# Graph layers and mixture of experts on one core: set-up by column groups, ScalarE pairs with a bank of their own, degrees made early, and tile 0 multiplied between the last pairs

## What is computed

```python
x = x + gnn(layernorm(x), (src, dst), edge_weight)      # two graph layers
x = x + ffn(layernorm(x))                               # 16 experts, the best 2 of each row

# gnn: h [3125, 256], 50000 edges, sorted by dst
ew  = clip(abs(edge_weight), 1e-6)
deg = segment_sum(ew, dst) + 1
dis = rsqrt(deg)
for W, b, g, be in two layers:
    xw  = h @ W
    agg = segment_sum((dis[src] * ew * dis[dst])[:, None] * xw[src], dst) + dis**2 * xw + b
    h   = relu(layernorm(agg) * g + be) + h
# ffn: gate (256 -> 16), top 2, softmax over the two, relu MLP 256 -> 512 -> 256 per expert,
#      y = x + weighted sum, layernorm of y
```

## Time and profile before

| what | value |
|---|---|
| median of 3 runs | 1250.4 us (1247.85 to 1251.97) |
| the profiled execution | 1253.59 us |
| its span, first to last instruction | 1251.9 us |
| mean granted TensorE clock | 0.954 |
| PE busy | 1102.1 us (88%), 6433 instructions |
| DVE busy | 720.1 us (58%) |
| POOL busy | 608.7 us (49%) |
| ACT busy | 341.6 us (27%) |

### The profile page before, as it was taken

The page is one execution under the profiler, slowest core; times in us unless marked ns, Lnnn a source line. Parts: engine busy times, 40 slices in busy tenths (PEclk is TensorE's granted clock), DMA queues, the critical chain, the costliest instruction groups (busy, mean ns, idle before and its releaser), DMA issues. The chain is left out here.

```text
span 1251.9 us, 19252 instructions
## 1 busy us (share of the span) xinstructions
PE 1102.1 (88%) x6433; PEld 952.7 (76%) x6436; DVE 720.1 (58%) x1970; ACT 341.6 (27%) x794; POOL 608.7 (49%) x625
## 2 busy tenths in 40 slices
PE   1675789799999999997799999999994599999967
PEld 1453568588888888886588888888883599999954
DVE  8978668903444444342427777777777355454536
ACT  1538332401111121111101111111211133343337
POOL 3777777777777777770001111111112355555525
PEclk9999978799999999998899999999996799999988
DMA  7999700033433433213045544535447422222236
GB/s 282 335 392 389 309 2 1 8 106 106 157 107 117 147 107 111 101 54 105 0 176 178 202 155 150 202 126 193 146 146 247 145 73 73 69 73 73 72 106 234
DMA packets 76335, 180.75 MB, mean 144 GB/s; under 512 B 28930, under 2 KB 58252, under 8 KB 66508
## 3 DMA queue, kind: packets, MB, share of 16 engines
q1 hardware_dynamic: 44984, 151.67, 33.6%
q0 software_dynamic: 19776, 15.76, 4.6%
q10 hardware_dynamic: 11476, 12.07, 3.0%
HBM read 122.12 MB, written 57.33 MB: 143 GB/s over the span
## 5 line engine op out<-in xcount | busy, mean ns | idle before, releaser
L458 POOL DMA_INDIRECT weights_by_cell<-w_cell,cell x391 | 413.0, 1056 | 140.5 <-issue 136.1
L1148 PE MATMUL ps<-x_rows,w 128*128 128x256 f32 x1300 | 296.4, 383 | 7.4 <-DMA w<-weights_by_cell 7.1
L1148 PE MATMUL ps<-w 128*128 128x256 f32 x1300 | 301.1, 385 | 1.1 <-ACT w L850 1.1
L1148 PEld LDWEIGHTS ps<-x_rows,w 128*128 128x128 f32 x1300 | 248.0, 192 | 41.2 <-DMA w<-weights_by_cell 7.9
L1148 PEld LDWEIGHTS ps<-w 128*128 128x128 f32 x1300 | 243.4, 192 | 32.7 <-ACT w L850 2.6
L508 POOL DMA_INDIRECT token_and_home_of_slot<-pair,slot_id x50 | 49.6, 992 | 346.7 <-DVE slot_id L779 339.1
L606 DVE TENSOR_TENSOR layer<-ps,w 128x1024 bf16<-128x1024 f32 x87 | 105.0, 1216 | 26.2 <-PE ps L987 26.1
L1466 DVE TENSOR_SCALAR hidt<-ps,b1t 128x128 f32<-128x128 f32 x232 | 65.3, 344 | 90.6 <-PE ps L1322 90.6
L1334 PE MATMUL ps<-w,hidt 128*128 (+1 forms) x464 | 109.8, 380 | 0.0
L1322 PEld LDWEIGHTS ps<-xt,w1s 128*128 128x128 f32 x880 | 106.9, 192 | 2.8
L1322 PE MATMUL ps<-xt,w1s 128*128 128x128 f32 x880 | 107.1, 275 | 0.0
(11 more groups left out here) (237 smaller groups left out, 1371.3 us busy)
## 6 DMA issues: line engine op xcount, KB each, us to landing
w<-weights_by_cell SPq DMA_DIRECT2D x49, 1600.0 KB, 6.9
weights_by_cell<-w SPq DMA_DIRECT2D x26, 1600.0 KB, 8.4
w<-in_L_ffn_w_dram SPq DMA_DIRECT2D x32, 512.0 KB, 8.8
weights_by_cell<-w_cell,cell POOLq DMA_INDIRECT x391
w<-in_x_dram ACTq DMA_DIRECT2D x1, 3072.0 KB
hot<-in_x_dram ACTq DMA_DIRECT2D x24, 128.0 KB, 2.1
normalised_rows<-hot ACTq DMA_DIRECT2D x24, 128.0 KB, 4.7
out_dram<-w SPq DMA_DIRECT2D x24, 128.0 KB
```

What stands on the lines that cost most here:

```text
L458: pool.indirect_dma_start(adj[:, :], bass.IndirectOffsetOnAxis(ap=cell[0:m, c:c + 1].bitcast(U32), axis=0), w_cell[0:m, n, half * CH + j:h ...
L1148: mm = pe.matmul(bank(k % 2, 0, D), ring[:, place_of(k), s * P:(s + 1) * P], tab[q][:, s, :], start=(s == 0), stop=(s == NT - 1))
```

## The change

- **Set-up by column groups.** The four groups of 128 columns are set up one by one (`part(g, j)`, 25 operations each). Group 0 is made before the first pair; groups 1 to 3 stand two operations at a time in pairs 4 to 43. The first edges and weights have DMAs and semaphores of their own. The keys of a group are made by PE (a matmul with `pick`). The limits stand behind pair 1, and the last four operations of group 0 behind them. POOL waits for `part_ready` of the chunk's group.
- **28 pairs on ACT** (17 from pair 20 to 52, then every fourth), with a PSUM bank, a `same` slot and a semaphore of their own; the other 70 share two banks.
- **Degrees early:** three one-hot operations per pair (pairs 4 to 53); W1 from block 88 on, every second block; `tab[0]` scaled one tile per block from block 140.
- **Tile 0 of the first layer** is multiplied into bank 6 between the last pairs, one square every second block from block 144.
- SP waits for POOL's own DMAs (`seconds`) against two numbers from a table, and not for `placed`.
- The blank tile is half as wide and read twice per write.
- **Experts, end:** the gates are made in block 6 of the experts, and 12 diagonal pairs (8 of them in `w1s`) are filled before the last stage; the other 13 are made by halves, one or two per tile.

```diff
-KBANKS = 3
+KBANKS, ACT_BANK = 2, 2
-HOT_FIRST, HOT_STEP = 4, 2
+HOT_FIRST, HOT_STEP = 4, 3
-P_MEAN, P_PASSED, P_SHIFT, P_DEG = 12, 14, 31, HOT_LAST + 4
-T_APPLY, T_TAB, TAB_STEP, T_DEG, T_SCALE = 66, 84, 3, 2 * P_DEG, 2 * P_DEG + 6
-
-ACT_FIRST, ACT_LAST, ACT_STEP = 20, 64, 4
+P_MEAN, P_PASSED, P_SHIFT, P_DEG = 14, 14, 22, HOT_LAST + 4
+T_APPLY, APPLY_STEP, T_TAB, TAB_STEP, T_DEG = 46, 4, 88, 2, 2 * P_DEG
+T_SCALE = max(2 * P_DEG + 6, T_TAB + TAB_STEP * NT + 2)
+T_TILE, TILE_STEP = T_SCALE + 4, 2
+P_GUARD = T_APPLY // 2 + 2
+ACT_PAIRS = tuple(range(20, 54, 2)) + tuple(range(56, PAIRED - 1, 4))
+DVE_PAIRS = tuple(p for p in range(PAIRED) if p not in ACT_PAIRS)
+SIDE, PART_OPS, PART_SPAN = 6, 24, 13
+SECONDS = 16 * (CH * ((CHUNKS + 1) // 2) - 1)
...
+def part_pair(g, j):
+
+    return 4 + (g - 1) * PART_SPAN + j // 2 + (j >= SIDE)
...
-XRING, DIAGS = 3, 4
+XRING, DIAGS, OWN_DIAGS = 3, 12, 4
...
                     if q == 0:
-                        sp.reg_load(reg, chunks_of[0:1, t:t + 1])
-                        sp.wait_ge(placed, sp.snap(reg, min_val=1, max_val=CHUNKS + 1))
+                        for j in range(2):
+                            sp.reg_load(regs[j], second_need[0:1, j, t:t + 1])
+                        for j in range(2):
+                            sp.wait_ge(seconds[j], sp.snap(regs[j], min_val=16 * CH, max_val=SECONDS))
+                            sp.sem_inc(cells_blank, 1)
...
                 pool.wait_ge(limits_ready, 1)
-                pool.wait_ge(cols_ready, 1)
                 for n in range(CHUNKS + 1):
                     if n < CHUNKS:
                         if n == 0:
                             load_needs(0)
+                        pool.wait_ge(part_ready, (n * CH + CH - 1) // SH + 1)
                         pool.wait_ge(w_ready, n + 1)
...
+                for j in range(21):
+                    part(0, j)
+                dve.wait_ge(cols_ready, 1)
...
                 pair(0)
                 pair(1)
-                link(dve.tensor_copy(work_i[:, :], dst_c))
-                link(dve.tensor_scalar(work_i[:, :], work_i[:, :], 7, None, ALU.logical_shift_right))
-                link(dve.tensor_copy(dst_hi, work_i[:, :]))
+                limits()
                 weigh(0)
-                link(dve.scalar_tensor_tensor(dst_lo, dst_hi, -float(P), dst_c, ALU.mult, ALU.add))
+                limits_back()
+                for j in range(21, PART_OPS + 1):
+                    part(0, j)
...
+                    if s >= T_TILE and (s - T_TILE) % TILE_STEP == 0 and (s - T_TILE) // TILE_STEP < NT:
+                        n = (s - T_TILE) // TILE_STEP
+                        if n == 0:
+                            pe.wait_ge(deg_ready, 1)
+                            pe.wait_ge(loaded[place_of(0)], 16)
+                        pe.wait_ge(tab_ready[0], n + 1)
+                        mm = pe.matmul(bank(6, 0, D), ring[:, place_of(0), n * P:(n + 1) * P], tab[0][:, n, :],
+                                       start=(n == 0), stop=(n == NT - 1))
...
-                if t + DIAGS < NT:
-                    act.wait_ge(y_ps, t + 1)
-                    for k in range(2):
-                        ins = act.activation(diag[:, t % DIAGS, k, :], ident[:, :], ACT.Copy, scale=top_w[:, k, t + DIAGS:t + DIAGS + 1])
-                    ins.then_inc(diag_ready, 1)
+                for j in range(halves_by(t), halves_by(t + 1)):
+                    d, k = DIAGS + j // 2, j % 2
+                    act.wait_ge(y_ps, d - DIAGS + 1)
+                    ins = act.activation(diag(d, k), ident[:, :], ACT.Copy, scale=top_w[:, k, d:d + 1])
+                    if k == 1:
+                        ins.then_inc(diag_ready, 1)
```

More of the change, by code:

```diff
@@ L212, in gnn @@
         odd_need = sb("odd_need", [P, SC * P // CH], U16)
-        dst_c = setup(COLS)
         key = setup(COLS)
-        work = [setup(COLS) for k in range(4)]
-        work_i = sb("work_i", [P, COLS], I32)
+        hi_f, shi, at_cell, rest = (setup(P) for k in range(4))
+        v_i, s_i, d_i = (setup(P, I32) for k in range(3))
         cell = sb("cell", [P, COLS], I32)
@@ L587, in _ @@
-                link(dve.tensor_scalar(fourth[:, :], fourth[:, :], 0.0, None, ALU.is_equal))
-                for c in range(SC):
-                    ins = dve.tensor_scalar(begun[:, c, :], iota_vt[:, :], edge_hi[:, c, 0:1], fourth[:, 0:1], ALU.is_ge, ALU.mult)
-                ins.then_inc(limits_in, 1)
-                dve.wait_ge(limits_ps, 1)
-                did(dve.tensor_scalar(chunks_of[:, :], bank(7, 0, VT), 1.0, None, ALU.add))
-                link(dve.tensor_copy(top_v[:, 0, :], bank(7, BANK // 2, BANK // 2 + SC * P // CH)))
@@ new lines, in _, with limits @@
+                dve.wait_ge(consts, CONSTS)
+                for j in range(21):
+                    part(0, j)
+                dve.wait_ge(cols_ready, 1)
+                def limits():
+                    dve.wait_ge(late_consts, LATE_CONSTS)
+                    dve.wait_ge(ends_in, 16 * 5)
+                    did(dve.tensor_copy(end_dst[:, :, 0], ends_i[:, :, 0, 0]))
+                    link(dve.tensor_copy(end_dst[:, :, 1], ends_i[:, :, 1, 1]))
+                    link(dve.tensor_tensor(edge_v[:, :, :], end_dst[:, :, :],
+                                           block_row[:, :].rearrange("p (c k) -> p c k", k=1).to_broadcast([P, SC, 2]), ALU.add))
+                    link(dve.tensor_copy(edge_vi[:, :, :], edge_v[:, :, :]))
+                    link(dve.tensor_scalar(edge_vi[:, :, :], edge_vi[:, :, :], 7, None, ALU.logical_shift_right))
+                    link(dve.tensor_copy(edge_hi[:, :, :], edge_vi[:, :, :]))
+                    did(dve.tensor_scalar(chunk_hi[:, :], edge_hi[:, :, 1], VT - 1.0, None, ALU.min))
+                    link(dve.tensor_scalar(block_i[:, :], block_i[:, :], CH - 1, None, ALU.bitwise_and))
+                    link(dve.tensor_copy(fourth[:, :], block_i[:, :]))
+                    link(dve.tensor_scalar(fourth[:, :], fourth[:, :], 0.0, None, ALU.is_equal))
+                    for c in range(SC):
+                        ins = dve.tensor_scalar(begun[:, c, :], iota_vt[:, :], edge_hi[:, c, 0:1], fourth[:, 0:1], ALU.is_ge, ALU.mult)
+                    ins.then_inc(limits_in, 1)
@@ L974, in _, with turn_part @@
-                mm.then_inc(turned_w, 1)
+                def turn_part(g):
+                    at = (3 if g == 0 else 7) * BANK
+                    pe.wait_ge(cast_ready, g + 1)
+                    if g >= 2:
+                        pe.wait_ge(part_ready, g)
+                    for half in range(2):
+                        pe.transpose(ps[:, at + half * P:at + (half + 1) * P], e_f[:, g, half * P:(half + 1) * P], ident[:, :])
+                    pe.wait_ge(ends_ready, g + 1)
+                    for half in range(2):
+                        a = at + 2 * P + half * SH
+                        pe.matmul(ps[:, a:a + SH], key_part[:, g, half * P:(half + 1) * P], pick[:, :], start=True, stop=True)
+                    pe.wait_ge(weights_ready, g + 1)
+                    pe.transpose(ps[:, at + 3 * P:at + 4 * P], e_w[:, g, :], ident[:, :]).then_inc(turned_w, 1)
@@ L999, in weigh @@
                             c = col(s, other)
-                            mm = pe.matmul(bank(4 + k % 2, a, a + 3), same[:, (s // 2) % MRING, s % 2, other, half * P:(half + 1) * P], w_parts[:, :, c],
+                            mm = pe.matmul(bank(4 + k % 2, a, a + 3), same[:, slot, s % 2, other, half * P:(half + 1) * P], w_parts[:, :, c],
                                            start=(other == 0), stop=(other == 1))
@@ L1116, in _ @@
                 pe.wait_ge(w_ready, CHUNKS)
-                for k in range(2 * VT):
+                for k in range(1, 2 * VT):
                     q, t = order(k)
@@ L1564, in _ @@
                 for k in range(2):
[L1565 removed]
+                    mm = pe.matmul(y_of(t), diag(t, k)[0:m, :], ya[0:m, k, t, :], start=(k == 0), stop=(k == 1))
                 mm.then_inc(y_ps, 1)
```

368 lines of the change are left out of this document (211 added, 157 removed).

## The result

| what | before | the changed kernel |
|---|---|---|
| median | 1249.76 us (20 runs, 1245.79 to 1253.11) | 1243.06 us (20 runs, 1235.6 to 1252.25) |
| ratio | | 0.9954, 95% interval [0.9934, 0.9974] |
| profiled execution | 1253.59 us | 1235.6 us, the fastest of its 20 |

The changed kernel is 6.7 us faster by the medians; 12.7 were forecast. Its runs spread over 16.7 us, those of before over 7.3. The three traces differ mainly in one stretch, and that shows where the time is.

What follows compares the result with a forecast made beforehand. The prediction took POOL's line of 391 placing DMAs to bound the first layer. POOL's earlier start (11 us) less holding (2) plus the last stage (3.7) gave 12.7 us off the 1250.4 median: 1237.7 us, range 1232 to 1250.

Steps and rivals of the forecast that it cites:

- POOL sets the first layer's end: First layer: it ends when POOL's line of 391 placing DMAs lets it; 9 us earlier (11 - 2).
- PE must begin tile 1 by 264: First layer: with placing 9 us earlier, tile 24 can be loaded by 561, so PE must begin tile 1 by 264.
- prediction's own signs of being wrong: POOL's last issue after 560, tile 24 over 16 us by its clock, or PE never idle for a first-layer load.
- Pairs, degrees, table, tile 0 are worth 0: pairs end at 204 to 250: Before tile 1: ScalarE pairs, early degrees, table and tile 0 are hidden by POOL, worth 0; DVE done at 204 to 250.
- Set-up: POOL starts 11 us earlier: Start of the kernel: setting up group 0 alone lets POOL begin at 21 to 22, 11 us earlier (bounds 8 and 13).
- Holding of issues: 2 us more: POOL's issues held by DVE operations during the pairs: 27 us in all, 2 more than before.
- rival with almost no holding: POOL's issues held 0.2 to 0.3 us per triple, POOL ends 15 to 18 us early, about 1230; chance 0.10.
- first rival: POOL falls into step with DVE, 0.8 us per triple, 15 us more in all: 1243.5 to 1250.7; chance 0.20.
- SP's new wait 0: First-layer loads: SP waiting for POOL's own DMAs instead of `placed` is worth 0 to 1 us, taken 0.
- Last stage 3.7 us: End of the experts: statistics every 0.92 us instead of 1.17 with one diagonal per tile; 3.7 us (bounds 2 and 4.2).
- The sum: Whole kernel: 9 us from the first layer plus 3.7 from the last stage, 12.7 us, giving 1237.7.

Runs made afterwards that it cites:

- act_early: Changed kernel with only the 12 pairs 20 to 42 on ScalarE, the other 16 back on DVE; 1226.89 us, ratio 0.9802 in the undisturbed third attempt.
- same_a: The changed kernel with no edit, run again for a second trace; 1243.74 us, ratio 0.9949.
- same_b: The changed kernel with no edit, a single run for a third trace; 1240.72 us.
- before_early: Kernel before with ACT_LAST 44 in place of 64, ScalarE's five late pairs going to VectorE; two disturbed attempts, ratios 0.9978 and 0.998.
- start_late: Changed kernel with POOL's first placing held back until chunk 3 is summed; 1244.31 us, ratio 0.9957.
- early_late_b: act_early with POOL's first placing held back as in start_late, second attempt; 1245.5 us, ratio 0.9969.

## Why the prediction was wrong, by its steps

- **"POOL sets the first layer's end"** fits the kernel before, by its wait at tile 24, and is right for act_early; for the changed kernel it is wrong. The prediction had asked where it turns: PE must begin tile 1 by 264. That held for a POOL line 9 us earlier. With the line as it came, 22.4 us earlier, the point is 249.6 (see act_early_c), and PE began at 260, 266 and 272. One of the prediction's own signs of being wrong came true by it: PE was never idle for a load in the first layer.
- **"Pairs, degrees, table, tile 0 are worth 0: pairs end at 204 to 250"** is the step that failed. They end at 259.5 to 271.8. I added up DVE's work (183 us; it was idle for 51 of the 93 us from pair 44 to 72) and gave it at most the idle time it had before, and never followed PE's and ACT's order through that stretch. With no ScalarE pair in it (act_early_c) the stretch is 33 us shorter and the kernel 16 us faster by the medians, so what was costed at 0 took away most of what POOL's line had gained. The row that would have shown it was in the trace of before: PE waited 14.0 us in 5 waits for ScalarE's Relu from 143 to 214 us, 2.8 for each pair that stands beside the table. The change has nine such pairs in the place of five, and a table step at every second column. In the other direction, tile 0 between the pairs was costed at 0 as well, and is worth about 8.
- **Set-up: POOL starts 11 us earlier**: 9.05. What ended POOL's last wait is the landing of a blanking DMA at 23.15, not the tables, which were ready by 21.4.
- **Holding of issues: 2 us more.** An issue that nothing holds takes 0.967. The excess over that of the first 150 issues was 24.8 us before and 12.3 after; 27 was forecast. This term is wrong in size and in sign. The rival with almost no holding (0.10) had the size per triple right, 0.25; its POOL line was to end 15 to 18 us early, and with what the start gave it ended 22.4 early. Of the 12.5 us between them 6.0 lie at 200 to 250 us (6.0 before, none after) and 3.6 at 40 to 60 (7.3 and 3.7, with ten and 13 issues). At 204 to 226, where the earlier trace rows have 13 issues in 18.27 us, no triples are left to be met, since they end with pair 53. Here are the windows of the placing DMAs in that stretch, after:

```profile
204.00:226.00 22.00, 16.82 (x18) 0.91 0.02 2
```

  The triples don't meet fewer issues: of the first 150, 45 begin inside a one-hot operation before and 48 after, with an excess of 12.7 and 8.6 us. The larger part comes from issues that fell into step with DVE. Before, 11 issues begin in the last 0.1 us of a comparison, just as the next one-hot operation starts, and are held for all of it: 8.8 us, at 43 to 63 and 192 to 225 us, among them. After, 42 issues begin inside a comparison and have 0.2 us of excess together. The first rival (0.20) expected more of just this; the kernel before had it, and the change, whose triples stand in one piece, has none. That the order of the operations is the reason would fit; no run took it apart.
- **SP's new wait 0**: the load of tile 25 went out at 548.27, 4.9 us after the last placing DMA ended; before 4.2. Within the 0 to 1 us given.
- **Last stage 3.7 us.** DVE's statistics come every 0.92 us, as said, where it was 1.17, but two of them now wait for PE, 1.30 us in the rows below and 0.68 at the last tile, and before they did not:

```profile
1206.67 0.42 DVE L1704 BATCH_NORM_STATS2 stats<-ps 128x6 f32<-128x256 f32 x1
1208.97 0.43 DVE L1704 BATCH_NORM_STATS2 stats<-ps 128x6 f32<-128x256 f32 x1 [1.30 <-PE ps L1671]
1209.91 0.42 DVE L1704 BATCH_NORM_STATS2 stats<-ps 128x6 f32<-128x256 f32 x1
```

  The stage itself is 2.2 to 2.6 us shorter by the executions compared above, within the bounds (2 and 4.2) but below the value taken. Counted from the second layer's start, filling included, the edit gives 0.9 us, which is not clear of the scatter: the term was too high, and by how much is open.
- **The sum.** By the executions' own stages: of the 9 us for the first layer same_a has 2.1, same_b 8.3 and the fastest 14.4, as its pairs end. Behind it they take 3.4 to 4.4 us less than the trace of before, in place of 3.7; but that trace is the longest there (652.7), and the two of before_early have 650.0 and 650.1. The median of 1243.1 lies in the range of 1232 to 1250 by luck: POOL's line gained over 13 us more than forecast and PE came too late to use it, and the two errors offset each other. It was none of my cases. A rival in which PE starts tile 1 too late was missing, although I had worked out the number for it.

## What to carry to other kernels

When an edit is costed at nothing since another engine covers it, work out by how much it may come late and price its own chain against that, engine by engine in program order; the busy time of one engine added up says only how early the end can be, not how late. An in-order engine that both helps in one loop (comparisons) and is a link in another (table) makes the loops wait for each other wherever they are interleaved: give it the help where it is no link. And before speeding up a line, find out which line is the bound: the same delay cost 0.6 us in one kernel and 18.6 in its neighbour.

## What was not expected of the hardware

- One kernel's time spread over 16.7 us. Of its three traces the longer ones are those in which more of the W1 products ran at the lower level of the clock (8, 10 and 16 of 25 sets, 1.91 us for 1.03). The first grant of 1.00 is recorded at 143, 144 and 193 us, so its moment alone does not order them. With PE filled through the same stretch (act_early_c) 3 sets ran at the lower level and the runs lie within 3 us.
- After each wait of 4.2 to 4.6 us for a load, PE's first eight products of a tile took 3.78 us in place of 1.89. The last tile behind such a wait took 1.8 to 3.1 us over the 13.17 of the others, after waits of 2.3 (start_late), 4.2 (act_early_c), 5.0 (early_late_b) and 7.1 us (before): a wait costs more than its own length.
- The holding works one way. An issue of a placing DMA that begins inside L635 took 1.37 us in the median (20 before) and up to 1.82. In 30 of the 50 cases L635 began under a running issue, and it took 0.68, at most 0.69. Issues that begin inside the comparison took 0.97 in the median (63).
- The trace view prints a clock of 1.00 where no grant is recorded; the length of a known matmul tells the level.
- In four jobs, on three chips of which one also gave an undisturbed job, the same program took 28% longer (1597 to 1608 us for 1250). PE stood for "issue" through the pairs, up to 15.7 us at a time, or for engines that stood so, and the granted clock was lower (0.89 to 0.91 for 0.94 to 0.97 in the mean); from the second layer on the program took 645 to 650 us, as elsewhere. The cause is open. A difference of 17 us vanished there. Only the kernel before, run beside each kernel, shows such a thing.
